# Retuning the cost table of a kernel's own list scheduler, and a second copy of its float32 scratch buffer

## The chip, the cores and the metric

The kernel runs on one core of a Trainium2 chip. The metric is the device time of one execution in microseconds (us). The core has five engines that this kernel uses: TensorE (PE) multiplies matrices, VectorE (DVE) and ScalarE (ACT) do elementwise work and read PSUM, GpSimd (POOL) does elementwise work in SBUF, and SyncE (SP) issues most DMAs; ACT issues the rest. Every engine works through its own instruction list in order, and the lists wait for each other by semaphores.

## What is computed

Two transformer layers over x (2 sequences of 1024 tokens, width 256, 16 heads of 16), with a context of 154 tokens:

```
# layer 0 (pre-norm)
h = ln1(x);  x = x + wo_sa(softmax(causal(rope(q(h)) rope(k(h)).T)) v(h))        # "sa"
h = ln2(x);  x = x + wo_ca(softmax(rope(q(h)) rope(k(ctx)).T) v(ctx))            # "ca"
h = ln3(x);  x = x + fc2(gelu_tanh(fc1(h)))
# layer 1
a = softmax(causal(q(x) k(ctx).T)) v(ctx)                                        # "la"
h = ln4(a + x);  out = h + W2(gelu(W1 h))
```

## The kernel before

**Tiling.** The 2 x 1024 tokens are cut into four chunks of 512 tokens (c = 0 to 3; two to a sequence). A chunk goes through stages made of small steps, and a step is a tuple such as ("proj", "qs", 3, 1). The steps that matter here:

- ("stats", norm, c, g): layer-norm statistics and scaling on DVE (L1156 to L1182); g = 1 carries the long part. ("tr", norm, c, g): the PE transposes the result (L854) and ACT copies it out.
- ("proj", kind, c, f): a projection of half the heads (f = 0 or 1); qs and ks are query and key of sa, qca the query of ca, qla that of la. PE multiplies (L881), ACT adds the bias into `rot` (L1303), DVE rotates it (not for qla) and splits it in bfloat16 parts (L1107 to L1117), POOL makes the third part (L1381). ("place", kind, c, f): SP issues six DMAs that lay the parts out by head in QA, KA or QC (L763). `rot` and `part` have two copies, so DVE, before it starts on the n-th projection, waits until the DMAs of the (n-2)-th have landed (`placed` in its list).
- ("max", att, c, hg, u): scores for the row maximum of a group of four heads (hg = 0 to 3): PE L968, then a DVE reduction L1200 from one of two PSUM banks. ("row", att, c, hg): the maxima are transposed (PE L982), rounded by DVE (L1211, L1212) and laid behind the queries by two small DMAs (SP, L770).
- ("exp", att, c, hg, g, h): scores once more with the maximum subtracted (L1001 or L1006, L1012 for la and ca) and the exponential on ACT (L1333). ("pv", ...): their product with the values into ps_o (L1043). ("evac", att, c, hg): ACT copies ps_o to `osb` (L1340). ("turn", att, c, hg): PE transposes osb (L1051), DVE divides (L1220, L1224).
- ("addatt", c, g): DVE adds la's result to x (L1138), ahead of ln4. ("lnout", c): DVE writes ln4's output (L1144, L1145).
- ("up", l, c, m) and ("down", l, c, m), m = 0 to 7: the two products of an MLP. The first is kept as float32r high and low halves: ACT computes the gelu twice (L1323 into `hid`, L1325 into `gel` in float32) and POOL subtracts (L1398). The input of an MLP is split in the same way in the tr steps of ln3 and ln4: ACT L1280 into `hup`, ACT L1287 into `gel`, POOL L1393. `gel` has one copy, so each ACT write of it waits until POOL has finished with the one before.

**What sets the order.** `order()` makes one list of 1721 steps, and each engine's instruction list is this list with the parts of other engines left out. It merges eleven threads of steps greedily: it keeps a running time per engine, adds the numbers of `COST` for each step (and of `LANDS` and `DMA_LATENCY` for what is landed later), asks `ready()` when the next step of each thread could start on PE, and takes the one with the least expected wait, ties going by `PRIORITY`. So a number in `COST` moves no work between engines. It changes what the scheduler believes of waits, and with that which steps stand beside which. The engines still wait by semaphores for what is really done.

Of the kernel before, what the change touches and what calls it, by code (L numbers as in the profile page):

```python
# [46 lines left out]
P = 128  # L47
B, LX, LY, E, H, FF = 2, 1024, 154, 256, 16, 1024
HD = E // H
CH = 512  # L50
# [5 lines left out]
KT = E // P  # L56
# [130 lines left out]
def split_weights():  # L187
# [10 lines left out]
    "wload": (("act", 0.6),), "wsave": (("act", 0.6),), "wsplit": (("act", 1.1), ("pool", 2.4)), "fetch": (("act", 2.4),),  # L198
    "stats": (("dve", 4.5),), "tr": (("pe", 0.6), ("act", 0.95)),
    "proj": (("pe", 1.9), ("act", 0.6), ("dve", 4.0)), "place": (("dma", 3.8),),  # L200
    "v": (("pe", 2.2), ("act", 0.55)), "wo": (("pe", 2.1), ("dve", 0.65)),
    "up": (("pe", 1.4), ("act", 1.4), ("pool", 1.3)), "down": (("pe", 1.41), ("act", 0.6)), "res": (("dve", 0.65),),
    "max": (("pe", 0.3), ("dve", 0.62)), "row": (("pe", 0.15), ("dve", 0.6), ("dma", 1.3)),
    "exp": (("pe", 0.25), ("act", 0.5)), "pv": (("pe", 1.0),), "evac": (("act", 0.5),),
    "turn": (("pe", 0.5), ("dve", 0.6)), "addatt": (("dve", 0.65),), "lnout": (("dve", 2.4),),
    "ctxk": (("pe", 1.3), ("act", 0.6), ("dve", 3.5), ("dma", 3.8)), "ctxv": (("pe", 2.6), ("act", 0.7)),
}
DMA_LATENCY = 2.2
LANDS = {"wload": 4.0, "wsave": 5.0, "fetch": 4.0}
LOW_LATER = 0.9  # L210
# [257 lines left out]
def build(nc, x, ctxT, sq, blocks, cols, rows, lnrow, ident, masks, trig, out):  # L468
# [14 lines left out]
    with ExitStack() as ctx:  # L483
# [40 lines left out]
        hT = sb("hT", [P, 2, KT, CH])  # L524
        gel = sb("gel", [P, CH])
        rot = sb("rot", [P, 2, CH])
# [33 lines left out]
        maskf = rot[:, :, :].rearrange("p a b -> p (a b)")[:, 0:MASKW]  # L560
        brow = gel[0:len(BIAS_ROWS), 0:E]
        bpart = [QC[0:len(BIAS_ROWS), i, 0:E] for i in range(3)]
# [665 lines left out]
        def _(act):  # L1228
# [12 lines left out]
            for s in ORDER:  # L1241
# [31 lines left out]
                if k == "tr":  # L1273
# [3 lines left out]
                    if what in ("ln3", "ln4"):  # L1277
                        half_of_input_free(act, s)
                        for f in range(KT):
                            act.activation(hup[:, 0, f, 2 * g * P:(2 * g + 2) * P], src[:, f, :], ACT.Identity,  # L1280
                                           bias=c0(what + "_b", f), scale=c0(what + "_g", f))
                        if low_nth[s] > 1:
                            act.wait_ge(s_low, low_nth[s] - 1)
                        dst = gel[:, :].rearrange("p (f n) -> p f n", f=KT)
                    if what in NORMS:
# [32 lines left out]
                elif k == "up":  # L1318
# [4 lines left out]
                    act.activation(hid[:, n % 2, 0, :], bank[:, :], gelu, bias=bias).then_inc(s_gelu, 1)  # L1323
                    act.wait_ge(s_low, low_nth[s] - 1)
                    act.activation(gel[:, :], bank[:, :], gelu, bias=bias).then_inc(s_chain_free[u % 2], 1)  # L1325
                elif k == "exp":
# [17 lines left out]
        def _(pool):  # L1344
# [22 lines left out]
            for s in ORDER:  # L1367
# [21 lines left out]
                elif k == "tr" and s[1] in ("ln3", "ln4"):  # L1389
                    cols = slice(2 * s[3] * P, (2 * s[3] + 2) * P)  # L1390
                    after_chain(pool, s)
                    half_of_input_free(pool, s)
                    pool.tensor_tensor(hup[:, 1, :, cols], gel[:, :].rearrange("p (f n) -> p f n", f=KT),  # L1393
                                       hup[:, 0, :, cols], ALU.subtract).then_inc(s_low, 1)
                elif k == "up":
                    n = up_nth[s]
                    after_chain(pool, s)
                    pool.tensor_tensor(hid[:, n % 2, 1, :], gel[:, :], hid[:, n % 2, 0, :],  # L1398
                                       ALU.subtract).then_inc(s_low, 1)
# [75 lines left out]
```

## Time and profile before

| | us |
|---|---|
| median of 3 runs | 1098.04 (1093.66 to 1100.06) |
| the profiled execution | 1102.32 |
| its span, first to last instruction | 1100.5 |
| PE busy | 902.2 (82%) |
| DVE busy | 599.0 (54%) |
| ACT busy | 481.1 (44%) |
| POOL busy | 174.4 (16%) |
| mean granted TensorE clock | 0.867 |

PE is busy for 82% of the span. Its time is what is to be explained: what stands in its list, and what it waits for. An idle stretch of another engine costs nothing by itself. A granted clock of 1.0 is TensorE's 2.4 GHz and 0.5 is 1.2 GHz; a value between is a mean over a stretch that had both.

### The profile page before, as it was taken

What the parts mean: (1) busy time and instruction counts of PE and PEld (TensorE: products, weight loads), DVE (VectorE), ACT (ScalarE), POOL (GpSimd) and SP (SyncE); (2) the same over time, 40 slices, a digit from 0 to 9 for tenths busy, and PEclk for the clock granted to TensorE, in tenths of its full rate; (3) what the DMA queues carried; (4) which work ended last, traced back from release to release, by engine and by line L of the source; (5) the groups of instructions that cost most, each with busy time, mean ns of one, the idle gap of its engine ahead of it and who ended that gap; (6) DMA issues with size and microseconds to landing.
All of it is one profiled execution on the core that took longest, in us unless ns stands there. A gap on an engine that the chain in (4) does not pass through costs nothing.

```text
span 1100.5 us, 14705 instructions
## 1 busy us (share of the span) xinstructions
PE 902.2 (82%) x5504; PEld 484.9 (44%) x5504; DVE 599.0 (54%) x1355; ACT 481.1 (44%) x926; POOL 174.4 (16%) x139
## 2 busy tenths in 40 slices
PE   2577877699889889878969886999886898898788
PEld 1233334244744256333337433743322473562377
DVE  3664764776467753368555777765206703515530
ACT  1224342145356555443443443256764444453543
POOL 4332000001300022001013101300000030230143
PEclk9768878598889989979889986999998798897888
DMA  8875343400640224239023602324003145062052
GB/s 301 231 207 140 50 89 57 58 2 20 163 59 14 28 53 139 32 69 112 2 29 110 102 3 29 116 77 59 2 20 41 18 131 81 26 158 30 1 173 96
DMA packets 60010, 86.08 MB, mean 78 GB/s; under 512 B 14726, under 2 KB 45602, under 8 KB 59938
## 3 DMA queue, kind: packets, MB, share of 16 engines
q1 hardware_dynamic: 46372, 38.99, 22.4%
q10 hardware_dynamic: 13568, 46.14, 12.3%
q8 instruction: 45, 0.74, 0.3%
q14 instruction: 25, 0.20, 0.1%
HBM read 47.08 MB, written 10.49 MB: 52 GB/s over the span
## 4 chain that ended last, share of the span: by engine, by line
PE 52%; DVE 14%; DMA 10%; ACT 9%; issue 8%; SPq 5%; POOL 2%; ACTq 0%; POOLq 0%; DVEq 0%
PE ps_o L1043 10%; PE ps_chain L905 8%; PE ps_max L968 7%; ACT probs L1333 5%; PE ps_exp L925 5%; PE ps_exp L1001 5%; DVE mcol L1200 5%; SPq L763 4%; DMA QA<-part 3%; PE ps_chain L881 3%; PE ps_exp L929 2%; PE ps_chain L889 2%; DMA QC<-part 2%; DMA stage<-in_blocks 2%; DVE swap L1107 2%
## 5 line engine op out<-in xcount | busy, mean ns | idle before, releaser
L1333 ACT ACTIVATE probs<-ps_exp 128x512 f32<-128x512 f32 (+3 forms) x544 | 261.2, 522 | 248.5 <-PE ps_exp L1006 88.5
L1200 DVE TENSOR_REDUCE mcol<-ps_max 128x3 f32<-128x462 f32 (+5 forms) x496 | 290.5, 625 | 123.2 <-PE ps_max L970 65.6
L968 PE MATMUL ps_max<-KA,QA 96*128 96x512 bf16 (+3 forms) x384 | 118.3, 360 | 53.5 <-DVE mcol L1200 28.2
L1001 PE MATMUL ps_exp<-QA,KA 98*128 98x512 bf16 (+3 forms) x384 | 119.1, 346 | 31.4 <-ACT probs L1333 24.9
L1381 POOL TENSOR_TENSOR part<-rot,part 128x512 bf16<-128x512 f32 (+1 forms) x36 | 40.5, 1126 | 568.4 <-DVE part L1117 568.4
L905 PE MATMUL ps_chain<-hup,ring 128*128 128x512 f32 x384 | 113.2, 436 | 3.7 <-ACT gel L1287 2.5
L1398 POOL TENSOR_TENSOR hid<-gel,hid 128x512 fp32r<-128x512 f32 x64 | 83.8, 1309 | 142.9 <-ACT gel L1325 142.9
L1323 ACT ACTIVATE hid<-ps_chain,col 128x512 fp32r<-128x512 f32 x64 | 44.1, 689 | 121.5 <-PE ps_chain L905 121.3
L1001 PEld LDWEIGHTS ps_exp<-QA,KA 98*128 98x128 bf16 x384 | 36.1, 99 | 125.6 <-ACT probs L1333 100.9
L1043 PE MATMUL ps_o<-probs,V 128*17 128x512 f32 (+3 forms) x768 | 85.8, 521 | 3.6 <-ACT probs L1333 2.6
L968 PEld LDWEIGHTS ps_max<-KA,QA 96*128 96x128 bf16 x384 | 37.4, 104 | 114.3 <-DVE mcol L1200 69.9
L905 PEld LDWEIGHTS ps_chain<-hup,ring 128*128 128x128 f32 x384 | 76.6, 210 | 22.1 <-issue 5.4
L1107 DVE TENSOR_TENSOR swap<-rot,sinT 64x512 f32<-64x512 f32 (+1 forms) x56 | 38.5, 688 | 85.6 <-ACT rot L1303 76.8
L925 PE MATMUL ps_exp<-ring,hid 128*128 128x256 f32 x512 | 76.8, 294 | 0.0
L925 PEld LDWEIGHTS ps_exp<-ring,hid 128*128 128x128 f32 x512 | 70.1, 195 | 6.5 <-issue 1.3
L970 PE MATMUL ps_max<-mask,idb 128*128 128x128 bf16 (+1 forms) x320 | 66.4, 235 | 0.0
L968 PE MATMUL ps_max<-KC,QC 96*128 96x154 bf16 x384 | 53.4, 253 | 12.6 <-DVE mcol L1200 7.9
L1004 PE MATMUL ps_exp<-mask,idb 128*128 128x128 bf16 x256 | 56.1, 229 | 0.0
L1303 ACT ACTIVATE rot<-ps_chain,col 128x512 f32<-128x512 f32 (+1 forms) x36 | 24.0, 669 | 64.6 <-PE ps_chain L881 54.0
L968 PEld LDWEIGHTS ps_max<-KC,QC 96*128 96x128 bf16 x384 | 31.8, 105 | 44.6 <-DVE mcol L1200 28.8
L1133 DVE TENSOR_TENSOR xb<-xb,ps_exp 128x512 f32<-128x512 f32 x16 | 10.2, 679 | 74.7 <-PE ps_exp L929 74.7
L1393 POOL TENSOR_TENSOR hup<-gel,hup 128x512 fp32r<-128x512 f32 x16 | 21.5, 1341 | 175.7 <-ACT gel L1287 175.7
(118 smaller groups left out, 1211.9 us busy)
## 6 DMA issues: line engine op xcount, KB each, us to landing
ring<-keep ACTq DMA_DIRECT2D x64, 512.0 KB, 3.3
QA<-part SPq DMA_DIRECT2D x72, 128.0 KB, 5.2
QC<-part SPq DMA_DIRECT2D x72, 128.0 KB, 5.2
keep<-ring ACTq DMA_DIRECT2D x8, 1024.0 KB, 5.3
KA<-part SPq DMA_DIRECT2D x48, 128.0 KB, 5.0
xb<-in_x SPq DMA_DIRECT2D x8, 512.0 KB, 6.2
stage<-in_blocks ACTq DMA_DIRECT2D x8, 512.0 KB, 8.6
out<-xb SPq DMA_DIRECT2D x4, 512.0 KB, 3.1
```

The lines of the kernel that those rows point to most:

```text
L905: mm = pe.matmul(bank[:, :], ring[:, n % RING, i, t * P:(t + 1) * P], hup[:, j, t, :], start=(i + j + t == 0), stop=(j + t == KT))
L925: pe.matmul(dst[t], hid[:, n % 2, 0, t * P:(t + 1) * P], ring[:, n % RING, j, 2 * P:4 * P], start=False, stop=False, skip_group_check=True)
L968: mm = pe.matmul(dst, q, kk, start=True, stop=not causal)
L970: mm = pe.matmul(bank[:, at0 + a0:at0 + a0 + w0], idb[:, :], mk, start=False, stop=True)
L1001: mm = pe.matmul(bank[:, q0:CH], KA[:, g // NT, hh, (g % NT) * P:(g % NT + 1) * P], QA[:, hh, q0:CH], start=True, stop=(r < 0))
L1004: mm = pe.matmul(bank[:, q0:q0 + P], idb[:, :], maskt, start=False, stop=True)
L1043: mm = pe.matmul(ps_o[p0:p0 + HD + 1, q0:CH], v, pr, start=first, stop=last, skip_group_check=True)
L1107: ins = dve.tensor_tensor(w[lo:lo + 64, a0:a0 + wd], r[hi:hi + 64, a0:a0 + wd], sinT[hi:hi + 64, t0:t0 + wd], ALU.mult)
L1200: dve.tensor_reduce(dst, src, AX.X, ALU.max).then_inc(s_max_done, 1)
L1323: act.activation(hid[:, n % 2, 0, :], bank[:, :], gelu, bias=bias).then_inc(s_gelu, 1)
L1333: act.activation(probs[:, n % 2, h, q0:CH], ps_exp[exp_nth[s] % 2][:, q0:CH], ACT.Exp).then_inc(s_exp_done, 1)
L1398: pool.tensor_tensor(hid[:, n % 2, 1, :], gel[:, :], hid[:, n % 2, 0, :], ALU.subtract).then_inc(s_low, 1)
```

## The change

It has two parts. The first edits the scheduler's numbers: a placing is now believed to land 1.3 us later (`LANDS`), a row of maxima 1.0 us earlier, and several durations go up or down by 0.05 to 0.5 us (`tr`, `proj`, `row`, `exp`, `evac`, `turn`). The second gives `gel` two copies, used in turn, so that ACT waits for the POOL subtraction before the last instead of the last. No instruction is added or taken away.

```diff
-    "stats": (("dve", 4.5),), "tr": (("pe", 0.6), ("act", 0.95)),
-    "proj": (("pe", 1.9), ("act", 0.6), ("dve", 4.0)), "place": (("dma", 3.8),),
+    "stats": (("dve", 4.5),), "tr": (("pe", 0.55), ("act", 1.15)),
+    "proj": (("pe", 1.8), ("act", 0.7), ("dve", 4.5)), "place": (("dma", 3.8),),
...
-    "max": (("pe", 0.3), ("dve", 0.62)), "row": (("pe", 0.15), ("dve", 0.6), ("dma", 1.3)),
-    "exp": (("pe", 0.25), ("act", 0.5)), "pv": (("pe", 1.0),), "evac": (("act", 0.5),),
-    "turn": (("pe", 0.5), ("dve", 0.6)), "addatt": (("dve", 0.65),), "lnout": (("dve", 2.4),),
+    "max": (("pe", 0.3), ("dve", 0.62)), "row": (("pe", 0.15), ("dve", 0.65), ("dma", 1.3)),
+    "exp": (("pe", 0.25), ("act", 0.56)), "pv": (("pe", 1.0),), "evac": (("act", 0.6),),
+    "turn": (("pe", 0.45), ("dve", 0.75)), "addatt": (("dve", 0.65),), "lnout": (("dve", 2.4),),
...
-LANDS = {"wload": 4.0, "wsave": 5.0, "fetch": 4.0}
+LANDS = {"place": 1.3, "ctxk": 1.3, "row": -1.0, "wload": 4.0, "wsave": 5.0, "fetch": 4.0}
...
-        gel = sb("gel", [P, CH])
+        gel = sb("gel", [P, 2, CH])
...
-                        if low_nth[s] > 1:
-                            act.wait_ge(s_low, low_nth[s] - 1)
-                        dst = gel[:, :].rearrange("p (f n) -> p f n", f=KT)
+                        if low_nth[s] > 2:
+                            act.wait_ge(s_low, low_nth[s] - 2)
+                        dst = gel[:, low_nth[s] % 2, :].rearrange("p (f n) -> p f n", f=KT)
...
-                    act.wait_ge(s_low, low_nth[s] - 1)
-                    act.activation(gel[:, :], bank[:, :], gelu, bias=bias).then_inc(s_chain_free[u % 2], 1)
+                    act.wait_ge(s_low, low_nth[s] - 2)
+                    act.activation(gel[:, low_nth[s] % 2, :], bank[:, :], gelu, bias=bias).then_inc(s_chain_free[u % 2], 1)
```

The first 27 steps of the list and one long stretch in the middle of chunk 2 and 3 stay as they were; elsewhere steps move by a few places, and at two places by much more.

**First place, PE, chunk 1's la attention.** Names: `w_sa_wq` marks the projection of sa's queries for chunk 3, second half, `w_l_wq` that of la's queries for chunk 1, `KC,QC 128x154` la's scores, `KA,QA` sa's, `idf,osb` a turn, `idf,mcol` a row, `idf,a_ctx` the transposes of ln4. Before, the projection stands behind the last of la's exps:

```order
L982 MATMUL ps_misc<-idf,mcol 16x128
L881 MATMUL ps_chain<-hT,w_sa_wq 128x512 x2
L1051 MATMUL ps_misc<-idf,osb 128x128 x4
L1012 MATMUL ps_exp<-QC,KC 32x512 x4
L1043 MATMUL ps_o<-probs,VA 17x512 x4
L1043 MATMUL ps_o<-probs,VB 17x512 x4
L1051 MATMUL ps_misc<-idf,osb 128x128 x4
L968 MATMUL ps_max<-KA,QA 128x128
```

Now it stands right behind the second projection of la's queries, and ahead of la's first scores:

```order
L881 MATMUL ps_chain<-hT,w_l_wq 128x512 x2
L982 MATMUL ps_misc<-idf,mcol 16x128
L881 MATMUL ps_chain<-hT,w_sa_wq 128x512 x2
L1051 MATMUL ps_misc<-idf,osb 128x128 x4
L968 MATMUL ps_max<-KC,QC 128x154 x16
L982 MATMUL ps_misc<-idf,mcol 16x128
L968 MATMUL ps_max<-KC,QC 128x154 x16
L1006 MATMUL ps_exp<-QC,KC 128x512 x2
L968 MATMUL ps_max<-KA,QA 128x128
```

The projection moved ahead by the whole of chunk 1's la attention, some 20 us of PE work.

**The same place on DVE, in the changed kernel.** `placed_qc0` is the landing of la's first queries, `max_ready` the scores:

```order
L1107 TENSOR_TENSOR swap<-rot,sinT 64x512 [waits chain_read1,placed_qc0]
L1107 TENSOR_TENSOR swap<-rot,sinT 64x512
L1111 TENSOR_TENSOR rot<-rot,cosT 128x512 [waits dve_chain]
L1113 TENSOR_TENSOR rot<-rot,swap 128x512 [waits dve_chain]
L1114 CAST part<-rot 128x512 [waits dve_chain]
L1116 TENSOR_TENSOR rot<-rot,part 128x512 [waits part0_ready]
L1117 CAST part<-rot 128x512 [waits dve_chain]
L1220 RECIPROCAL rec<-ps_misc 128x16 [waits misc_ready]
L1224 TENSOR_TENSOR a_sa<-ps_misc,rec 128x4x64 [waits dve_chain]
L1200 TENSOR_REDUCE mcol<-ps_max 128x3 [waits max_ready] x5
```

The rotation of the moved projection stands ahead of la's first reductions.

**Second place, PE, the end of the last attention.** Before, the first transposes (`idf,a_ctx`, ln4 of chunk 2) stand among the last products of chunk 3, and the MLP of chunk 2 follows:

```order
L1043 MATMUL ps_o<-probs,VA 17x512 x4
L854 MATMUL ps_chain<-idf,a_ctx 128x128 x4
L1051 MATMUL ps_misc<-idf,osb 128x128 x4
L854 MATMUL ps_chain<-idf,a_ctx 128x128 x4
L1043 MATMUL ps_o<-probs,VB 17x512 x4
L1051 MATMUL ps_misc<-idf,osb 128x128 x4
L905 MATMUL ps_chain<-hup,ring 128x512 x12
```

Now the last head group is one of chunk 2, and `idf,a_sa` is ln4 of chunk 3, whose MLP comes first:

```order
L1043 MATMUL ps_o<-probs,VA 17x512 x4
L1051 MATMUL ps_misc<-idf,osb 128x128 x4
L1043 MATMUL ps_o<-probs,VB 17x512 x4
L1051 MATMUL ps_misc<-idf,osb 128x128 x4
L854 MATMUL ps_chain<-idf,a_sa 128x128 x8
L905 MATMUL ps_chain<-hup,ring 128x512 x12
```

The MLPs of chunks 2 and 3 have changed places, and between the turn whose result ln4 needs and ln4's transposes stand one product and one turn.

## Rows read from the trace of the kernel before

**Rows 1.** The page: busy time of the engines, with shares and instructions.
```profile
PE 902.2 (82%) x5504; PEld 484.9 (44%) x5504; DVE 599.0 (54%) x1355; ACT 481.1 (44%) x926; POOL 174.4 (16%) x139
```
**Rows 2.** Waits of PE: who waited for whom, us in total, times, longest.
```profile
PE ps_max L968 <- DVE mcol L1200: 40.0, 74, 5.9
...
PE ps_max L968 <- DMA QA<-part: 24.8, 6, 6.5
...
PE ps_max L968 <- DMA QC<-part: 4.0, 4, 1.5
...
PE ps_exp L1001 <- DMA QA<-mrow: 2.4, 2, 2.0
...
PE ps_exp L1006 <- DMA QC<-mrow: 0.8, 1, 0.8
```
**Rows 3.** Windows: from:to, length, busy (instructions) of PE, PEld, DVE, ACT, POOL, clock, DMA.
```profile
550.00:577.50 27.50, 18.72 (x108) 10.17 (x109) 14.91 (x42) 12.34 (x26) 3.65 (x3) 0.81 0.22 30
660.00:687.50 27.50, 17.76 (x82) 9.16 (x81) 21.10 (x50) 8.95 (x16) 5.01 (x4) 0.61 0.22 29
```
**Rows 4.** Timeline, PE, products of up steps: start, us, ... xcount [idle before <-releaser].
```profile
418.51 1.55 PE L905 MATMUL ps_chain<-hup,ring 128*128 128x512 f32 x6
...
681.48 2.96 PE L905 MATMUL ps_chain<-hup,ring 128*128 128x512 f32 x6
```
**Rows 5.** Timeline, PE, the two longest waits of scores for placed queries in chunks 2, 3.
```profile
478.49 0.29 PE L968 MATMUL ps_max<-KA,QA 96*128 96x128 bf16 x1 [4.87 <-DMA QA<-part]
...
852.15 0.95 PE L968 MATMUL ps_max<-KC,QA 96*128 96x154 bf16 x6 [6.47 <-DMA QA<-part]
```
**Rows 6.** DMA issues: line, count, KB, median us from issue to landing.
```profile
QA<-mrow SPq DMA_DIRECT2D x48, 4.0 KB, 1.8
```
**Rows 7.** Timeline, the entry of chunk 1's first MLP.
```profile
570.66 1.15 POOL L1381 TENSOR_TENSOR part<-rot,part 128x512 bf16<-128x512 f32 x1 [55.18 <-DVE part L1117]
...
573.06 1.02 ACT L1287 ACTIVATE gel<-ps_chain,col 128x256 f32<-128x256 f32 x2 [3.73 <-POOL hup L1393]
...
574.41 0.39 PE L1001 MATMUL ps_exp<-QA,KA 98*128 98x256 bf16 x1 [7.17 <-ACT probs L1333]
```
**Rows 8.** Timeline, chunk 1's ln4 and the projection that the change moves.
```profile
658.05 2.01 PE L881 MATMUL ps_chain<-hT,w_sa_wq 128*128 128x512 f32 x4
...
664.26 3.84 SPq L763 DMA_DIRECT2D QA<-part  x6
...
666.14 1.09 PE L1051 MATMUL ps_misc<-idf,osb 128*128 128x128 f32 x4 [3.40 <-DVE a_ctx L1224]
...
672.89 0.29 PE L968 MATMUL ps_max<-KA,QA 96*128 96x128 bf16 x1 [5.66 <-DMA QA<-part]
...
673.70 1.38 DVE L1182 TENSOR_SCALAR a_ctx<-xb,mv,nw 128x256 f32<-128x256 f32 x4
```
**Rows 9.** Timeline, PE, chunk 1's first la queries and their first scores.
```profile
614.60 2.02 PE L881 MATMUL ps_chain<-hT,w_l_wq 128*128 128x512 f32 x4
...
626.91 0.58 PE L968 MATMUL ps_max<-KC,QC 96*128 96x154 bf16 x6 [0.64 <-DMA QC<-part]
```
**Rows 10.** Timeline, DVE, a rotation whose second-last placing had not landed.
```profile
509.76 1.39 DVE L1107 TENSOR_TENSOR swap<-rot,sinT 64x512 f32<-64x512 f32 x2 [1.69 <-DMA QC<-part]
```
**Rows 11.** Timeline, the end of the last attention and the second last MLP entry.
```profile
1037.38 1.11 PE L1051 MATMUL ps_misc<-idf,osb 128*128 128x128 f32 x4 [3.00 <-ACT osb L1340]
...
1049.46 2.45 DVE L1182 TENSOR_SCALAR a_sa<-xb,mv,nw 128x256 f32<-128x256 f32 x4
...
1066.31 1.17 PE L905 MATMUL ps_chain<-hup,ring 128*128 128x512 f32 x4 [2.52 <-ACT gel L1287]
...
1068.67 3.78 PE L905 MATMUL ps_chain<-hup,ring 128*128 128x512 f32 x8 [1.19 <-POOL hup L1393]
```
**Rows 12.** Waits of ACT for POOL.
```profile
ACT gel L1287 <- POOL hup L1393: 6.6, 7, 3.7
ACT gel L1325 <- POOL hid L1398: 4.9, 4, 2.9
```

More of the change, by code:

```diff
@@ L560, in build @@
         maskf = rot[:, :, :].rearrange("p a b -> p (a b)")[:, 0:MASKW]
-        brow = gel[0:len(BIAS_ROWS), 0:E]
+        brow = gel[0:len(BIAS_ROWS), 0, 0:E]
         bpart = [QC[0:len(BIAS_ROWS), i, 0:E] for i in range(3)]
@@ L1392, in _ @@
                     half_of_input_free(pool, s)
-                    pool.tensor_tensor(hup[:, 1, :, cols], gel[:, :].rearrange("p (f n) -> p f n", f=KT),
+                    pool.tensor_tensor(hup[:, 1, :, cols], gel[:, low_nth[s] % 2, :].rearrange("p (f n) -> p f n", f=KT),
                                        hup[:, 0, :, cols], ALU.subtract).then_inc(s_low, 1)
@@ L1397, in _ @@
                     after_chain(pool, s)
-                    pool.tensor_tensor(hid[:, n % 2, 1, :], gel[:, :], hid[:, n % 2, 0, :],
+                    pool.tensor_tensor(hid[:, n % 2, 1, :], gel[:, low_nth[s] % 2, :], hid[:, n % 2, 0, :],
                                        ALU.subtract).then_inc(s_low, 1)
```

## Prediction

> **What bounds the kernel now.** First the page's busy times: PE works 902.2 of 1100.5 us, no other engine over 55% [rows 1]. No instruction is added or removed, so the time moves only if PE's idle time or its clock moves. Second the waits of PE by releaser. The two large kinds are the DVE reduction of the score before (40.0 us in 74 small waits, inherent in two PSUM banks) and queries not yet placed: 24.8 us in 6 waits plus 4.0 in 4 [rows 2]. The rows of maxima are almost never waited for: 2.4 us in 2 waits plus 0.8 in 1 [rows 2]. Third the windows: around the two worst stalls the granted clock is 0.81 and 0.61, against 0.867 on the mean [rows 3]. So a stall costs twice, once as idle time and again as work at the lower of the two levels: six up products take 1.55 us in full flow and 2.96 behind the second stall [rows 4].
>
> For each wait I take how much PE work lies between a step and the step that needs it (the sum of PE's own times of the steps between, from this trace, in the old order and in the new). What does not cover the chain's length is idle time. These distances are my estimates.
>
> **1. Placings believed later.** The numbers now make the scheduler put 1.3 us more between a projection and its first scores. The distances grow: chunk 2's second sa projection from 14.6 to 16.8 us of work, where PE idles 4.87 now, so -2.2; chunk 3's ca projection from 6.0 to 6.9, idle 6.47, so -0.9 [rows 5]. The other places, all among the small waits of [rows 2]: chunk 2's first sa projection -1.0 (its whole wait), chunk 0's sa -0.8 and ca -0.5, la of chunks 0, 2 and 3 -0.4, -0.7 and -1.1. Sum: 3.1 + 1.0 + 1.3 + 2.2 = 7.6, so -7.6. Bounds: 0 (what moved in between is missing elsewhere) and -10.
>
> **2. Rows believed 1.0 us earlier.** The exps that read a row come closer behind it. A row's DMAs land 1.8 us after issue [rows 6], and the issue stands about 1.2 us behind PE's transposition, 3.0 in all; the nearest exps now stand at 2.5 to 3.9 us of work. Some ten of them could miss by up to 0.5 us, and others profit from being elsewhere. Bounds 0 and +3.2 (the present waits of this kind, doubled); I take +0.5, nearer to zero since most distances still cover.
>
> **3. Entry of chunk 1's first MLP.** Here PE stands 7.17 us because ACT is blocked 3.73 us before writing `gel`, behind two POOL operations, the first for a projection (570.66) [rows 7]. That projection is now about 6 us earlier, and with two copies ACT waits for neither. What is left is the chain transposition, four ACT copies, exp: about 1.8 of the 7.17. So -5.4. The stretch behind it runs at 0.81 [rows 3]; if it returned to nearly 1.0, 18.72 us of work would give back 3. Together -8.4, bounds -4 (only the 3.73 goes) and -10.
>
> **4. The moved projection (first place of the change).** It is `qs` of chunk 3, second half. It now stands 6.3 us of PE work behind the first la projection of chunk 1, with which it shares a copy of `rot`. From a la projection's end to its scores on PE passes 10.3 us (616.6 to 626.9) [rows 9]. So DVE waits for that landing, as it did for 1.69 us in the one such row [rows 10], until PE could be 10.3 us on; then it rotates for 4.5 us, until 14.8. La's reductions stand behind it in DVE's list, and PE has two banks, so PE stops at the third group of scores. And SP has the placing's six DMAs, 3.84 us of issue [rows 8], ahead of the rows of maxima. I get PE's first la exp at 21.3 us and the next scores at 22.3 against 10.9 us of work there: 11.4 idle, where now 3.9 are. Then ln4 of chunk 1: four reductions in between make its chain from turn to transposition 9.7 us, against 1.6 us of work that is left to cover it, since the projection and its scores have gone: about 8 idle. Now PE idles 3.40 ahead of the turn, which counts to the attention's 3.9, and 5.66 for the placed queries [rows 8], 5.8 with the small gaps beside it; that wait goes, and the statistics show in its place. Balance: 11.4 - 3.9 = +7.5 at la, 8 - 5.8 = +2 at ln4, +9.5 in all; and some 2 us of full-rate work more falls to the lower clock, which by the two rates of [rows 4] costs +2. So +11.5. Bounds: +3 (DVE catches up while PE has other steps, and the 5.66 pays for half) and +16 (both stalls whole, and 0.61 as granted clock over 27 us instead of 0.81 [rows 3]).
>
> **5. The end (second place).** ln4 of chunk 3 now comes first and right behind its turn: turn 0.8, addition 1.4, turn 0.7, statistics 5, transposition at 8.3, four ACT copies of 1.0 each, up products at 12.9, against 2.9 us of work: 10 idle. Now 3.00 is lost there [rows 11]. So +7, and 1.5 for the clock. The last evacuation stands ahead of the last exp on ACT, -1.2. The second entry loses 2.52 and 1.19 now [rows 11], waiting for `gel` and the subtraction; with two copies most of that goes, and with the clock I take -4. Sum +3.3, bounds -3 and +8. The statistics here take 1.38 us for the last four operations if POOL is quiet, as in [rows 8], and 2.45 if it is not, as in [rows 11]; POOL should be quiet, as the other chunk's MLP is not running.
>
> That difference fits the Trainium skill, page "SBUF — State Buffer", section "Who interferes with whom": DVE's two-port modes and GpSimd take the same pair of ports in turns. By that page alone the stall at the end would be the shorter of the two; the sum is the same.
>
> **6. Output layer norm and chunk 3's ln3.** The work between chunk 3's output projection and its transposition falls from 5.1 to 1.3 us: 4.8 idle for 1.7, less 1.5 for la waits of chunk 2 that it takes the place of: +1.6. Elsewhere small moves of 0.3 to 1.0 us, -2.7 in all, bounds -5 and +2.
>
> **7. Two copies elsewhere.** ACT's waits for POOL at `gel` are 6.6 and 4.9 us in the whole span [rows 12], the 3.73 of part 3 among them. In the flow of an MLP PE never waits for them, so I cost the rest at nothing; what hides it is PE's work on 18 products a step. The float32r subtraction keeps its own place on POOL.
>
> **Sum.** -7.6 + 0.5 - 8.4 + 11.5 + 3.3 + 1.6 - 2.7 = -1.8 us. From the profiled execution, 1102.3, that gives 1100.5. That execution stood 4.3 over the median of the runs, 1098.0, so the median would be 1096.2, rounded to 1096.5.
>
> **Rivals.** *A, the forecast:* gains and losses cancel. *B, the moved projection is covered.* If DVE's wait ends before PE runs out of la scores (the other steps there, a turn and sa scores, use DVE little) part 4 is +3, and if ln4 of chunk 3 at the end finds its turn early, part 5 is 0: -1.8 - 8.5 - 3.3 = -13.6, median 1084. For it: DVE is only 54% busy [rows 1], so the stretch around may leave it slack. Against: both projections share one copy, and 6.3 is less than 10.3. *C, DVE is blocked for its full length.* The wait for la's first landing, behind the moved projection, decides as soon as that landing is later than PE's third group of la scores; then part 4 is +16 and, with part 5 at +8 by the same pattern of an exposed norm, the sum is +7.4, median about 1105.5. For it: the clock of 0.61 after just such a stall [rows 3]. Against: the distances may be larger than I sum, since PE works slower at the lower clock and so covers more. *D, the numbers do nothing real:* the gains of part 1 are taken back at the next wait for a reduction, since DVE's 40.0 us stay [rows 2]; then the sum is -1.8 + 7.6 = +5.8, median 1104, at the slow bound of no change.
>
> On the clock the Trainium skill, page "TensorE: Matmul & The Clock Gate", section "HAM oscillation — how this bites in real kernels", says that an array left waiting between bursts falls to its low clock, so that each burst begins slow. The two rates in [rows 4] agree. Without the clock's terms (-3 in part 3, +2 in part 4, +1.5 and some -1.5 in part 5) the sum would be -0.8, nearly the same; with new stalls of 8 to 11 us the page speaks for C.
>
> **How the numbers follow.** A measurement of this kernel can tell about 0.5%, 5.5 us, from no change: 1092.5 to 1103.5. Chances: A 0.36, B 0.34, C 0.20, D 0.10. A's own spread is some 5 us, so 0.06 of it lies below the middle and 0.03 above. B reaches into the middle with 0.04, C with 0.02, and D lies half in it. Faster 0.06 + 0.30 = 0.36, same 0.27 + 0.04 + 0.02 + 0.05 = 0.38, slower 0.03 + 0.18 + 0.05 = 0.26. The independent bounds of parts 1, 3, 4 and 5 give about +-12 us; the range takes B's 1084 with 2 us and C's 1105.5 with the outer bound of part 4: 1082 to 1114.
>
> **What would show it.** Right for 1: the waits of `ps_max` for QA and QC fall from 28.8 us to below 20. For 3: no idle time over 3 us at chunk 1's first MLP entry. For 4: DVE waits several us for QC's placing ahead of a rotation in chunk 1's la attention, and PE waits for `mcol` there over 5 us; a granted clock near 0.6 behind it. For 5: 8 to 11 us of idle PE ahead of the last `a_sa` transpositions, statistics at 1.38. For 7: ACT's waits for POOL fall from 11.5 to under 3. Wrong it would be if DVE never waits at the moved projection (B), or if idle time at it exceeds 15 us (C), or if the waits for placings fall and those for `mcol` rise by as much (D).

## The result: slower by 1.8%, outside the range

The changed kernel takes 1116.9 us (median of 4 runs, 1110.48 to 1119.29) against 1096.01 us for the kernel before in the same comparison. The ratio is 1.0177, interval [1.0121, 1.0234]. The forecast was 1096.5 in a range of 1082 to 1114. The nearest rival, C (DVE blocked behind the moved projection), named 1105.5.

### The profile page after: what moved, and what is told of

Read it like the earlier page. It is cut to its first block, busy times and chain, and to the rows that moved or that the text cites. A ratio compares the mean times of both kernels' runs of the same rounds, so it can differ in the third digit from the quotient of the medians.

```text
span 1116.5 us, 14707 instructions
## 1 busy us (share of the span) xinstructions
PE 907.6 (81%) x5504; PEld 487.6 (44%) x5504; DVE 601.2 (54%) x1355; ACT 478.6 (43%) x926; POOL 175.9 (16%) x139
## 4 chain that ended last, share of the span: by engine, by line
PE 55%; DVE 17%; DMA 10%; ACT 9%; SPq 4%; issue 3%; POOL 1%; ACTq 0%; POOLq 0%; DVEq 0%
PE ps_o L1043 11%; PE ps_max L968 8%; PE ps_chain L905 8%; DVE mcol L1200 6%; ACT probs L1333 5%; PE ps_exp L1001 5%; PE ps_exp L925 4%; PE ps_chain L881 4%; PE ps_chain L889 3%; SPq L763 3%; DMA QA<-part 3%; PE ps_exp L929 2%; PE ps_exp L1006 2%; PE ps_chain L854 2%; DMA stage<-in_blocks 2%
## 5 line engine op out<-in xcount | busy, mean ns | idle before, releaser
L1200 DVE TENSOR_REDUCE mcol<-ps_max 128x1 f32<-128x512 f32 (+5 forms) x496 | 291.9, 626 | 121.7 <-PE ps_max L968 60.3
L968 PE MATMUL ps_max<-KA,QA 96*128 96x512 bf16 (+3 forms) x384 | 121.6, 365 | 45.5 <-DVE mcol L1200 28.9
L905 PE MATMUL ps_chain<-hup,ring 128*128 128x512 f32 x384 | 109.1, 424 | 8.0 <-ACT gel L1287 5.1
L1398 POOL TENSOR_TENSOR hid<-gel,hid 128x512 fp32r<-128x512 f32 x64 | 85.7, 1340 | 139.7 <-ACT gel L1325 139.7
L968 PEld LDWEIGHTS ps_max<-KA,QA 96*128 96x128 bf16 x384 | 38.7, 105 | 106.6 <-DVE mcol L1200 75.2
L1043 PE MATMUL ps_o<-probs,V 128*17 128x512 f32 (+3 forms) x768 | 82.3, 501 | 3.1 <-ACT probs L1333 2.8
L905 PEld LDWEIGHTS ps_chain<-hup,ring 128*128 128x128 f32 x384 | 73.3, 201 | 24.3 <-issue 6.5
L968 PE MATMUL ps_max<-KC,QC 96*128 96x154 bf16 x384 | 55.3, 259 | 14.8 <-DVE mcol L1200 11.7
L968 PEld LDWEIGHTS ps_max<-KC,QC 96*128 96x128 bf16 x384 | 32.6, 107 | 47.4 <-DVE mcol L1200 34.7
L1220 DVE RECIPROCAL rec<-ps_misc 128x16 f32<-128x16 f32 x48 | 12.2, 253 | 74.5 <-PE ps_misc L1051 74.4
```

Source lines behind the costliest of these rows:

```text
L905: mm = pe.matmul(bank[:, :], ring[:, n % RING, i, t * P:(t + 1) * P], hup[:, j, t, :], start=(i + j + t == 0), stop=(j + t == KT))
L968: mm = pe.matmul(dst, q, kk, start=True, stop=not causal)
L1043: mm = pe.matmul(ps_o[p0:p0 + HD + 1, q0:CH], v, pr, start=first, stop=last, skip_group_check=True)
L1200: dve.tensor_reduce(dst, src, AX.X, ALU.max).then_inc(s_max_done, 1)
L1398: pool.tensor_tensor(hid[:, n % 2, 1, :], gel[:, low_nth[s] % 2, :], hid[:, n % 2, 0, :], ALU.subtract).then_inc(s_low, 1)
```

## The profile after

First the page's busy times and PE's waits by releaser, as in [rows 1] and [rows 2]; columns as there.

```profile
span 1116.5 us, 14707 instructions
...
PE 907.6 (81%) x5504; PEld 487.6 (44%) x5504; DVE 601.2 (54%) x1355; ACT 478.6 (43%) x926; POOL 175.9 (16%) x139
```
```profile
PE ps_max L968 <- DVE mcol L1200: 44.6, 70, 6.0
...
PE ps_chain L854 <- DVE a_ctx L1182: 12.0, 3, 4.5
...
PE ps_chain L854 <- DVE a_sa L1182: 9.6, 2, 5.8
PE ps_max L968 <- DMA QA<-part: 9.2, 4, 4.8
PE ps_exp L1001 <- DMA QA<-mrow: 7.4, 1, 7.4
...
PE ps_max L968 <- DMA QC<-part: 2.9, 3, 1.4
```

The edit does what it says: the waits for placed queries fell from 28.8 us [rows 2] to 9.2 + 2.9 = 12.1. The time went elsewhere: 44.6 for 40.0 on the reductions, 7.4 for 2.4 on a row, and two lines for the statistics of ln2, ln3 and ln4 (12.0 and 9.6, where the trace of before has 4.4 and none).

The largest of the waits that fell, 6.47 us ahead of chunk 3's first ca scores [rows 5], only changed its name. A transposition of chunk 2's ca result now stands ahead of these scores, and waits 5.05 us for a divide that DVE does behind the rotation of the same projection (PE and DVE, start, us, instruction, [idle before <- releaser]):

```profile
845.26 0.63 PE L1051 MATMUL ps_misc<-idf,osb 128*128 128x128 f32 x4 [0.32 <-DVE a_ctx L1224]
...
849.83 0.43 DVE L1117 CAST part<-rot 128x512 bf16<-128x512 f32 x1
...
850.46 0.42 DVE L1224 TENSOR_TENSOR a_ctx<-ps_misc,rec 128x256 f32<-128x256 f32 x1
850.94 1.11 PE L854 MATMUL ps_chain<-idf,a_ctx 128*128 128x128 f32 x4 [5.05 <-DVE a_ctx L1224]
852.36 0.95 PE L968 MATMUL ps_max<-KC,QA 96*128 96x154 bf16 x6 [0.30 <-DMA QA<-part]
```

From the end of that turn to the scores pass 6.5 us, as before; one transposition of 1.11 us has moved into the gap.

The place of the moved projection, chunk 1's la: timeline, PE and DVE (start, us, instruction, [idle before <- releaser]).

```profile
620.02 0.28 PE L982 MATMUL ps_misc<-idf,mcol 128*16 128x128 f32 x1 [2.58 <-DVE mcol L1208]
620.14 3.64 PE L881 MATMUL ps_chain<-hT,w_sa_wq 128*128 128x512 f32 x4
...
624.05 0.56 PE L968 MATMUL ps_max<-KC,QC 96*128 96x154 bf16 x6
624.60 1.39 DVE L1107 TENSOR_TENSOR swap<-rot,sinT 64x512 f32<-64x512 f32 x2 [3.67 <-ACT rot L1303]
...
629.63 3.46 DVE L1200 TENSOR_REDUCE mcol<-ps_max 128x3 f32<-128x462 f32 x6
630.32 1.11 PE L968 MATMUL ps_max<-KC,QC 96*128 96x154 bf16 x6 [5.70 <-DVE mcol L1200]
...
675.54 1.76 PE L854 MATMUL ps_chain<-idf,a_ctx 128*128 128x128 f32 x7 [4.17 <-DVE a_ctx L1182]
```

The first la scores are there at 624.05, but DVE rotates the moved projection until 629.1 and then divides for a turn before it reduces them, and PE stands 5.70 us. What the prediction had wrong is visible too: DVE's rotation was released by ACT's `rot`, not by a landing. Against [rows 8] the same projection takes 3.64 us instead of 2.01: it runs at about half the rate behind the 2.58 us wait.

The end of the last attention, as in [rows 11].

```profile
1043.34 0.66 PE L1051 MATMUL ps_misc<-idf,osb 128*128 128x128 f32 x4
...
1051.31 1.38 DVE L1182 TENSOR_SCALAR a_sa<-xb,mv,nw 128x256 f32<-128x256 f32 x4
1052.11 1.97 PE L854 MATMUL ps_chain<-idf,a_sa 128*128 128x128 f32 x8 [5.76 <-DVE a_sa L1182]
...
1055.97 1.05 ACT L1287 ACTIVATE gel<-ps_chain,col 128x256 f32<-128x256 f32 x2
...
1057.11 1.19 PE L905 MATMUL ps_chain<-hup,ring 128*128 128x512 f32 x2 [3.04 <-ACT gel L1287]
```

From the turn of chunk 3 to its first up product pass 13.8 us, for which the prediction said 12.9. The statistics took 1.38, as said for a quiet POOL. Windows (from:to, length, busy of PE, PEld, DVE, ACT, POOL, granted clock, DMA): the first is la of chunks 2 and 3 in the changed kernel, the second the same microseconds before.

```profile
990.00:1028.00 38.00, 32.21 (x159) 11.60 (x161) 16.25 (x36) 10.54 (x19) 0.00 (x0) 0.53 0.16 17
```
```profile
990.00:1028.00 38.00, 29.83 (x201) 10.33 (x204) 22.32 (x63) 14.81 (x28) 0.00 (x0) 0.83 0.22 23
```

PE is busier and does fewer instructions, 159 instead of 201: 38 us almost wholly at the lower level. No part of the prediction had this.

## The experiments

The lists of steps before and after hold the same steps up to three points: step 848 (chunk 1's last ca scores), step 1189 (chunk 3's first sa products) and step 1412 (chunk 3's first ca scores). So the old and the new list can be joined there. Where such a joined list is used, both lists are computed by the file's own scheduler (`old` with the numbers of before, `new` with those of after), and all lines of the profile behind `order()` are 28 to 35 higher (L996, L997 or L1003 is L968 of before). "Two copies" is the change's second part, which all kernels have but e0 and e2. Reference for most is e1: two copies and nothing else.

**e1: two copies, old list.**

```diff
-LANDS = {"place": 1.3, "ctxk": 1.3, "row": -1.0, "wload": 4.0, "wsave": 5.0, "fetch": 4.0}
+LANDS = {"wload": 4.0, "wsave": 5.0, "fetch": 4.0}
```
(and `COST` as before)

> The second part alone: two copies of gel, the list of steps as before. Theory (the changed kernel loses at the moved projection and at the end, and gains at chunk 1's first MLP entry by both parts together): only ACT's 3.73 us wait and the second entry's 2.52 and 1.19 go, so -4 to -7 us against before, 1089 to 1092. Rival (the second copy gives nothing, since PE stands for ACT's work itself and POOL's projection step stays in front of the subtraction): within 2 us of before. Either way the idle stretch of 7.17 us ahead of the exps of chunk 2 shortens to about 3.5 by the theory and stays at 7 by the rival.

Measured: 1082.54 us, ratio 0.9876 [0.9852, 0.9900], -12.4 us. It is the fastest kernel of the study, and the change's second half alone. The gain is larger than the 4 to 7 us of the theory.

**e0: the kernel before once more.** No edit.

> The kernel before once more, for a trace of the same day as the others. The record of before shows a granted clock of 0.95 in its undisturbed stretches, and those of all kernels since show 1.00. Theory (that is a property of the one recorded execution): now 1.00, with a time of 1091 to 1099 and a span some 7 us below the first record. Rival (it belongs to this list of steps): 0.95 again.

Measured, in one run: 1095.06 us, span 1093.2, clock 0.907. The first record was a long execution with a clock of 0.867; where it shows 0.93 from 290 to 390 us, this one shows 0.97 and 1.4 us less PE time (from 960 to 980 us it is 0.95 and 1.00). So the theory holds.

```profile
290.00:390.00 100.00, 90.50 (x643) 41.47 (x642) 70.82 (x147) 56.01 (x110) 7.73 (x7) 0.93 0.31 54
```
```profile
290.00:390.00 100.00, 89.12 (x650) 40.08 (x648) 71.30 (x151) 56.14 (x110) 7.23 (x6) 0.97 0.29 49
```

So the traces from here on are compared with e0 and e1. Chunk 1's first MLP entry, e0 (ACT, PE), then e1 (ACT, PE):

```profile
567.50 1.02 ACT L1287 ACTIVATE gel<-ps_chain,col 128x256 f32<-128x256 f32 x2 [3.87 <-POOL hup L1393]
...
568.85 0.39 PE L1001 MATMUL ps_exp<-QA,KA 98*128 98x256 bf16 x1 [7.33 <-ACT probs L1333]
```
```profile
563.45 1.04 ACT L1287 ACTIVATE gel<-ps_chain,col 128x256 f32<-128x256 f32 x2
...
564.82 0.28 PE L1001 MATMUL ps_exp<-QA,KA 98*128 98x256 bf16 x1 [3.34 <-ACT probs L1333]
```

ACT's wait of 3.87 is gone and PE's falls by 3.99; PE waits 1.63 us for placed queries 8 us later, where e0 doesn't. ACT's waits for POOL at `gel` are 6.7, 6.5 and 0.5 us in e0, and none is left in e1:

```profile
ACT gel L1287 <- POOL hup L1393: 6.7, 7, 3.9
ACT gel L1325 <- POOL hid L1398: 6.5, 7, 2.9
```
```profile
ACT rot L1303 <- POOL part L1381: 2.3, 1, 2.3
ACT VA L1312 <- POOL ring L1387: 2.0, 1, 2.0
ACT hT L1287 <- POOL ring L1387: 0.9, 1, 0.9
```

The two spans differ by 10.9 us. By the pages PE's idle time (span less busy) is 200.0 and 191.0 us, its busy time 893.2 and 891.3. By place the picture is another. Of the idle time 5.1 us lie between 480 and 680 us, but PE's own time there is 4.7 longer in e1, so that e1 is ahead by only 2.8 us at step 1583, in the middle of chunk 2's la. The other 8.1 us come behind it: 1.6 of idle time, mostly at the last MLP's entry, 1.6 in the last MLP (25.6 us of PE time in e0, 24.0 in e1) and 4.9 in la of chunks 2 and 3, where e0 ran partly at the lower level (granted clock 0.66 from 980 to 1000 us). No step there writes `gel`, and e0 is one execution, so it is not shown that this last part belongs to the second copy. The first record of before is as slow behind step 1583 (109.7 us, e0 111.0, e1 102.9).

```profile
980.00:1000.00 20.00, 16.80 (x98) 7.47 (x98) 10.56 (x24) 6.21 (x12) 1.16 (x1) 0.66 0.49 52
```

**e2: new list, one copy.** `COST` and `LANDS` of after, everything else of before.

> The first part alone: the new list of steps, one copy of gel. Theory: in the new list the projection is 6 us earlier and POOL free at chunk 1's entry, so one copy costs there at most 1 us, but at the two last entries 2 to 3 each: +3 to +6 us against the changed kernel, about 1121. Rival (the whole gain at chunk 1's entry was the second copy): +8 to +10 against the changed kernel, about 1126.

Measured: 1114.18 us, ratio 1.0166 [1.0136, 1.0195], not to be told from the changed kernel; theory and rival both said more. So in the new list the second copy is worth nothing that can be told, where it gives 12.4 us in the old one. The trace says why for chunk 1's entry: with the new list and one copy, ACT's longest waits at `gel` are 1.5 and 0.5 us, since the projection that held POOL stands 6 us earlier. There both parts of the change went for the same wait. Why nothing of the rest is left is not shown.

```profile
ACT gel L1325 <- POOL hid L1398: 3.8, 5, 1.5
ACT gel L1287 <- POOL hup L1393: 3.3, 7, 0.5
```

**e5, e3, e4: the new list in one stretch only.**

```diff
+    return new[:848] + old[848:]                   # e5
+    return old[:848] + new[848:1189] + old[1189:]  # e3
+    return old[:1412] + new[1412:]                 # e4
```

> Two copies of gel, the new list up to step 848 (chunk 1's last ca scores, where both lists hold the same steps), the old list behind it. It holds nearly all of the retimed placings of part 1 of the prediction but neither the moved projection nor the new end. Theory A (the prediction's part 1 stands, 4 to 6 us are gained by placings no longer waited for): 1077 to 1079. Theory B (what is gained at the placings is given back at other waits in the same stretch, since against the kernel with two copies alone the changed kernel's trace has 2 to 3 us more idle time there): within 2 us of it, 1081 to 1085.

> Two copies of gel, the old list with steps 848 to 1189 of the new one: chunk 3's first query projection ahead of chunk 1's ln3, and the moved projection; first part and end are the old ones. Theory (the moved projection costs what the changed kernel's trace loses against the kernel with two copies alone, 16 to 18 us from chunk 1's la queries to chunk 2's ln2, less the 5 gained ahead): +9 to +13 against the kernel with two copies alone, 1092 to 1096. Rival (rotation, placing and rows waited for are mostly covered, as the case B of the prediction, and undoing it gave only 7): +2 to +5, 1085 to 1088.

> Two copies of gel, the list of before up to chunk 3's first ca scores (step 1412, where both lists hold the same steps) and the new list from there. Theory 1 (the end costs by itself): the trace of the changed kernel loses 15 us against before from there on, 7.5 at ln3 of chunk 3, 6 in la of chunks 2 and 3 at the low clock, and 10 at the exit less the 3 that the second copy gives. So +12 to +17 against the kernel with two copies alone. Rival (the losses at the end follow from the clock that the earlier stretch leaves behind, not from the list): under +8, the low stretch at la of chunks 2 and 3 missing and only the exit's idle time there.

| | us | ratio to before | against e1 |
|---|---|---|---|
| e5, first stretch | 1084.92 | 0.9920 [0.9890, 0.9949] | +2.4 |
| e3, middle | 1097.59 | 1.0019 [0.9991, 1.0047] | +15.0 |
| e4, end | 1107.23 | 1.0101 [1.0074, 1.0129] | +24.7 |
| changed kernel | 1116.9 | 1.0177 [1.0121, 1.0234] | +34.4 |

The last column is a difference of medians; e5 was timed on another chip than e1, and by the ratios the four are +4.8, +15.7, +24.6 and +33.0, each good to some 4 us. e5 is what theory B said, e3 lies 2 us and e4 8 us above their theories. The middle and the end lose.

The traces say where. The table has the time on PE of each stretch, in one execution of each kernel, between the steps at which the lists can be joined (e8 and e12 are described below; at step 1583 the new list differs by one step):

| | to 848 | to 1189 | to 1412 | to 1583 | to the end |
|---|---|---|---|---|---|
| e0, before | 534.8 | 199.6 | 102.6 | 140.7 | 111.0 |
| e1, two copies | 534.8 | 197.9 | 102.6 | 139.6 | 102.9 |
| e5, first stretch | 532.4 | 200.5 | 102.6 | 140.1 | 103.1 |
| e3, middle | 533.3 | 211.7 | 103.4 | 140.0 | 103.1 |
| e8, placing's number | 529.5 | 214.4 | 103.3 | 143.4 | 102.9 |
| e4, end | 534.5 | 198.5 | 102.5 | 142.1 | 124.2 |
| e12, exit | 534.8 | 197.7 | 102.6 | 139.7 | 114.4 |
| changed kernel | 533.3 | 209.8 | 102.8 | 142.0 | 124.2 |

In the changed kernel the differences to e1 are -1.5, +11.9, +0.2, +2.4 and +21.3, and their sum is the whole. The three differences of the table above sum to 42, 8 more: e5 shows +2.4 for that -1.5, e3 +15.0 for 11.9, e4 24.7 for 23.7. e5 is 2.4 us ahead at step 848 and loses it by step 1189, over steps that stand as in e1. So the retimed placings gain nothing that lasts (theory B).

In e5 and in the changed kernel one place shows how the gain is given back, chunk 0's last sa group. The timeline of SP's queue and of PE, first of the changed kernel:

```profile
148.83 4.46 SPq L757 DMA_DIRECT2D KC<-part  x6
153.33 1.25 SPq L770 DMA_DIRECT2D QA<-mrow  x2
```
```profile
155.74 0.61 PE L1001 MATMUL ps_exp<-QA,KA 98*128 98x512 bf16 x1 [7.41 <-DMA QA<-mrow]
```

And of e0, SP's queue and PE:

```profile
148.93 3.97 SPq L757 DMA_DIRECT2D KC<-part  x6
152.94 1.25 SPq L770 DMA_DIRECT2D QA<-mrow  x2
```
```profile
150.42 1.09 PE L1051 MATMUL ps_misc<-idf,osb 128*128 128x128 f32 x4 [2.27 <-DVE mrow L1212]
155.35 0.61 PE L1001 MATMUL ps_exp<-QA,KA 98*128 98x512 bf16 x1 [1.79 <-DMA QA<-mrow]
```

The row's DMAs stand in SP's queue behind six of the context's keys, in both kernels, and SP gets to them at the same time. PE has done 3 us more of its list by then, waits 0.72 + 7.41 instead of 2.27 + 1.79, and goes on at 155.74 instead of 155.35.

In e3 the rows of the moved projection are those of the changed kernel: waits of 2.58 and 4.92 us in la and 4.16 at ln4. Taking out the steps that only stand in another order, e3 is 7 us ahead of e1 at 595 us and 12 us behind at 743, so the stretch with the moved projection costs 19 to 20 us, some 14 of it idle time. That is gross: part of it takes back the 7 us gained ahead of it.

**e6, e7: the moved projection undone at step 1003.**

```diff
+    head = new[:1003]
+    return head + [s for s in old[:1189] if s not in head] + new[1189:]   # e6
+    return head + [s for s in old if s not in head]                       # e7
```

> The changed kernel with the first place undone: behind chunk 1's second la projection the list of before is followed up to step 1189, where both lists hold the same steps, and then the new one again. Theory 1 (the moved projection is the loss): the changed kernel's trace loses 16 us from there to chunk 2's ln2 against before; DVE does not wait for QC's placing ahead of a rotation, the idle 5.70 and 2.58 us are gone, and the time is 12 to 16 us below the changed kernel, about 1103. Rival (the stretch is lost to the clock in any case, as before with 0.61): at most 5 us below, 1112 or more.

> Two copies of gel, the new list up to chunk 1's second la projection (step 1003), the old one behind it: the moved projection and the new end are both undone. Theory 1 (these two places are the whole loss): below the kernel with two copies alone by what the stretch ahead gains in the changed kernel's trace, 5 to 8 us by chunk 1's first MLP, so 1075 to 1079. Rival (the time is lost again at the joint, since the projection then waits for its turn behind la as before): 1082 to 1088.

Measured: e6 1109.82 us (1096.82 to 1114.38 in 10 runs), ratio 1.0093 [1.0058, 1.0128], 7 below the changed kernel (9 by the ratios) instead of 12 to 16; e7 1086.04, ratio 0.9926 [0.9897, 0.9955], 3.5 above e1 (5.5 by the ratios) instead of 3 to 7 below, as its rival said. The joint has a fault of its own, as e7's timeline shows below: the new list has used up chunk 3's scores by step 1003, and nothing is left to cover the placing of la's queries.

```profile
620.16 0.95 PE L997 MATMUL ps_max<-KC,QC 96*128 96x154 bf16 x6 [5.42 <-DMA QC<-part]
```

The 5.70 us are replaced by 5.42. So these two don't give the price of the moved projection, and e3 gives it only together with this: e7, with the projection at its old place, is 10 us ahead of e1 at step 1003 and 1 us ahead at step 1189, so it loses 9 us there, where e3 loses 19. The gain ahead of that point, visible in the traces of e3 and of the changed kernel too, is borrowed: it comes from having spent that cover. The moved projection by itself costs between 10 and 20 us; no run parts it from the rest.

**e8: of all numbers only the placing's.**

```diff
-LANDS = {"wload": 4.0, "wsave": 5.0, "fetch": 4.0}
+LANDS = {"place": 1.3, "ctxk": 1.3, "wload": 4.0, "wsave": 5.0, "fetch": 4.0}
```

> Two copies of gel and of all numbers only the 1.3 us for a placing. Its list has the moved projection but the old end (MLP of chunk 2 first). Theory (the placing's number brings the moved projection, other numbers the new end, and the new end is the larger loss): 1085 to 1095, well below the changed kernel. Rival (any list with placings believed later loses as much by new waits for reductions): 1105 or more.

Measured: 1100.97 us (1093.67 to 1107.34), ratio 1.0046 [1.0009, 1.0083], between the two expectations: 18.4 above e1. Its list moves the projection too, but is the old one from step 1583 on, and its trace is 16.5 us behind e1's between steps 848 and 1189 and equal to it at the end (table above). So the placing's number alone brings the middle's loss, and the end's needs the other numbers.

**e12, e9, e10, e11: the end taken apart.** e12 has the old list up to the last turn of chunk 3 and behind it chunk 3's ln4 and MLP first; e9 takes the new list from step 1583, in the middle of chunk 2's la; e10 has only steps 1412 to 1583 of the new one; e11 is e4 with the exps, products, evacuation and turn of chunk 2's last la group behind chunk 3's statistics.

```diff
+    first = [s for s in old[:old.index(("turn", "la", 3, 3)) + 1] if s[:3] != ("tr", "ln4", 2)]
+    return first + [s for s in new if s not in first]                     # e12
+    head = old[:1583]
+    return head + [s for s in new if s not in head]                       # e9
+    head = old[:1412] + new[1412:1583]
+    return head + [s for s in old if s not in head]                       # e10
+    both = old[:1412] + new[1412:]                                        # e11
+    last = [s for s in both if s[:4] == ("exp", "la", 2, 3) or s[:4] == ("pv", "la", 2, 3)]
+    rest = [s for s in both if s not in last]
+    for s in (("evac", "la", 2, 3), ("turn", "la", 2, 3)):
+        rest.remove(s)
+        last.append(s)
+    i = rest.index(("stats", "ln4", 3, 1)) + 1
+    return rest[:i] + last + rest[i:]
```

> Two copies of gel, the old list up to the last turn of la in chunk 3, only without chunk 2's ln4 transpositions, and behind it chunk 3's statistics, transpositions and MLP first and chunk 2's last: the exit exposed by itself, with chunk 2's and 3's la as in the old list. Theory (the new end costs twice: the exposed ln4 chain, about 10 us idle, and apart from it 11.5 us of la work more at the low clock, which comes from the new interleaving of chunks 2 and 3): +9 to +12 against the kernel with two copies alone, 1092 to 1095, and la of chunks 2 and 3 keeps its 52 us of PE time. Rival (the exit is the whole loss of 24 us, the low clock being its companion): 1103 to 1108.

> Two copies of gel, the old list up to step 1583, in the middle of chunk 2's la attention, the new one behind it: chunk 3's la ahead of chunk 2's last group, and the MLP of chunk 3 first. Theory (the exit of the last attention is exposed as part 5 says, with 10 us idle): +10 to +14 against the kernel with two copies alone, 1093 to 1097. Rival (the exit costs only together with the low clock of the attention ahead of it, which the steps before 1583 bring): under +6, 1088 or less.

> Two copies of gel, the old list with steps 1412 to 1583 of the new one: chunk 3's ln3 with 1.3 us of work ahead of its transposition instead of 5.1, and chunk 2's la queries and scores around it; the end is the old one. Theory (the stretch costs what its own trace shows, 5 us of idle time at ln3 and 3 around it): +7 to +9 against the kernel with two copies alone, about 1090. Rival (the prediction's +1.6): 1084. If this and the run with the new end alone add up to the 25 us of both together, the two are independent; if they fall 5 us or more short of it, the two meet in the low clock of chunk 3's la attention.

> The kernel with the new end alone, and in it one thing changed: the exps and products of chunk 2's last la group stand behind the turn, the addition and the statistics of chunk 3, so that some 4 us of work cover ln4's chain. Theory (the exposed chain is most of the loss at the end): the 5.8 us of idle time ahead of the transposition fall to 1 or 2, and the time falls by 4 to 6 us against the new end alone, to about 1102. Rival (most of the loss is the low clock in chunk 3's la attention ahead of it, which this doesn't touch): under 2 us, 1105 or more; a low clock of 0.50 between 985 and 1025 us of the trace stays in either case.

| | us | ratio to before | against e1 |
|---|---|---|---|
| e12, exit alone | 1096.08 | 1.0000 [0.9970, 1.0031] | +13.5 |
| e10, ln3 and la of chunk 2 | 1085.47 | 0.9918 [0.9887, 0.9948] | +2.9 |
| e9, from step 1583 | 1108.58 | 1.0123 [1.0072, 1.0174] | +26.0 |
| e11, e4 with the exit covered | 1101.95 | 1.0067 [1.0043, 1.0091] | +19.4 |

e9, e10 and e12 were timed on other chips than e1; by the ratios they are 27.0, 4.6 and 13.6 above it. e12 lies 1.5 us above its theory, far from its rival; e10 is at its rival's value and not at its theory's; e9 is far above both.

The exit by itself costs 13.5 of e4's 24.7 us. In e12's timeline of PE it is idle time:

```profile
1021.98 0.66 PE L1080 MATMUL ps_misc<-idf,osb 128*128 128x128 f32 x4 [0.72 <-ACT osb L1369]
1029.90 1.97 PE L883 MATMUL ps_chain<-idf,a_sa 128*128 128x128 f32 x8 [7.26 <-DVE a_sa L1211]
1034.90 1.62 PE L934 MATMUL ps_chain<-hup,ring 128*128 128x512 f32 x3 [3.04 <-ACT gel L1316]
```

That is 11.0 us, where e1 waits 2.48. The other 11 are the clock in la of chunks 2 and 3. PE's own time in all steps of these two stages, summed from the traces, is 52.3 us in e1, 52.4 in e12, 63.8 in e4 and in the changed kernel (64.1 in e11). With the old interleaving it is 52.3 to 54.0 in six executions and 58.0 in e0, with either half of the new one 54.0 (e10) and 58.7 (e9). The windows of e12 first, then e4:

```profile
980.00:1000.00 20.00, 14.77 (x120) 6.42 (x124) 14.55 (x32) 6.62 (x12) 0.00 (x0) 0.97 0.33 36
1000.00:1020.00 20.00, 15.62 (x96) 4.41 (x89) 8.94 (x34) 9.76 (x18) 0.00 (x0) 0.86 0.01 1
```
```profile
980.00:1000.00 20.00, 17.13 (x91) 6.88 (x91) 11.32 (x24) 4.58 (x9) 0.00 (x0) 0.55 0.29 31
1000.00:1020.00 20.00, 17.36 (x78) 4.96 (x74) 5.62 (x14) 5.69 (x11) 0.00 (x0) 0.51 0.00 1
```

So the low clock does not belong to the exit; most of it comes with the new interleaving of the two chunks. e10, which has the first half of it, loses little. e9 has the second half but brings a wait of 5.49 us of its own for chunk 3's placed queries at the joint, so it can't price that half. e11 covers the chain with 4 us of work: the wait for ln4's statistics falls from 5.76 to 1.16, and the time by 5.3 us, as its theory says for this step; the low clock stays. That the exposed chain is most of the loss at the end, which the same theory says, does not hold: the two are of one size. The row of e11's timeline:

```profile
1037.63 1.30 PE L889 MATMUL ps_chain<-idf,a_sa 128*128 128x128 f32 x8 [1.16 <-DVE a_sa L1217]
```

## Why the prediction was wrong, point by point

The forecast was -1.8 us; the span of the changed kernel is 23.3 us above e0's. By stretch, with the parts that can be placed (the rest, +0.5 of part 2 and -2.7 of small moves, can't):

| | said | changed kernel against e0 |
|---|---|---|
| to step 848 (part 1's waits there) | -4.9 | -1.5 |
| to step 1189 (parts 3 and 4) | +3.1 | +10.2 |
| to the end (part 1's other waits, parts 5 and 6) | +2.2 | +14.7 |

- **Part 1, -7.6: failed.** The waits for placings fell (in e5 from 32.1 us in e1 to 27.1, and at chunk 2's second sa projection by the 2.2 said), but e5 as a whole is at +2.4. The step that failed is taking each wait's shortening as time gained. The next wait takes it up: in chunk 0 behind it stands a DVE and SP chain that is not moved, and PE only comes to it earlier (155.35 and 155.74 us); at chunk 3's ca the 6.47 became 5.05 + 0.30.
- **Part 2, +0.5.** The waits for rows rose from 3.2 us to 7.4 + 1.6, beyond the upper bound of +3.2. But the 7.41 is the wait just named, which also takes the place of another 2.27. No run has the row's number alone; its price is open.
- **Part 3, -8.4.** Right in mechanism and place. In e1 the second copy takes 3.99 of the 7.33, as the bound of 3.73 said; in the changed kernel the gap is gone. The 3 us of clock are not seen in e1: PE's own time from step 848 to 1003 is 77.4 us in e0 and 77.7 in e1. And e2 shows that the two parts are alternatives there, and e7 that the earlier projection is paid for at la's queries. Part 7 priced the second copy elsewhere at nothing; in the old list it brings 12.4 us in all, against some 8 by parts 3 and 5.
- **Part 4, +11.5: right in sign; with part 3 it gives +3.1, and the stretch lost 10.2.** In e3's trace it is 19 to 20 gross, beyond the bound of 16, of which some 9 are lost in e7 too, where the projection has its old place; so whether the part by itself was within its bounds is open. DVE's wait for QC's placing, from which the price was worked out, did not occur; what blocks is the rotation itself, on DVE from 624.60 to 629.0. Missing in the sum are the 2.58 ahead of the projection, its run at half rate (3.64 for 2.01) and the wait of 3.40 for chunk 2's ln2 later (3.54 in e3), where e0 and e1 have none over 1 us.
- **Part 5, +3.3: the chain was right, 9.5 us of idle time in the changed kernel for 10 said.** The term was mis-sized twice. The exit costs 13.5 (e12), not 7 + 1.5 - 1.2. And the -4 for the second entry was too much: two copies leave 2.02 and 0.58 of the 3.71 there. The 11.5 us of la work at the low clock (63.8 for 52.3) were in no term; this is the largest single miss.
- **Part 6, +1.6 for ln3: +2.9 in e10 (4.6 by the ratios),** near the outer end of what a comparison of this size can tell. The idle time ahead of ln3's transposition is 3.83 us in the changed kernel, for 4.8 said.
- **The rivals.** The cases took their sum from part 1's gain and added clock in small lumps. Without part 1, by the prediction's other terms alone, the forecast is +5.8, rival D's 1104, which had 0.10. D's mechanism, a gain taken back at the next wait, holds. Of C's, DVE is blocked by the rotation and not by a landing. Neither rival has the low clock in la, and neither gives 1117.
- **The record.** The trace of before was an execution 7 us above the later median and at a lower clock. The long waits that the prediction used are in e0 again within 0.6 us, so this moved no step. Two readings were off and carry no term: the second window of [rows 3] is not at one of the two worst stalls (6.47 us at 852 [rows 5] is longer than its 5.66), and 1096.2 was rounded up to 1096.5.

What stays open: why the granted clock stays at its lower level in la of chunks 2 and 3 with the new interleaving and not with the old. From 980 to 1020 us neither has a wait over 1.5 us (e4 and e1). Also open is what the second copy gives behind step 1583, beyond the 3.2 us at and in the last MLP, and what the moved projection costs by itself.

## What to carry to other kernels

A wait that is removed is worth only the distance to the next thing that is already late on the same chain; follow that chain (DVE, then SP's queue) before the gain is booked. Where a scheduler's numbers change, look first for the largest move, and ask whose turn on DVE it takes: 4.5 us of rotation ahead of the reductions that PE needs held PE for 5.70 us at one place, and the retimed placings saved nothing that lasted. A cheap structural edit (a second buffer) is to be timed apart from a retuning: here it gives 12.4 us alone and nothing together with the new numbers, which the joint change, slower by 21 us, could not show.

## What the runs showed of the hardware

TensorE's granted clock can stay at its lower level while PE is busy: 0.53 over 38 us with 32.21 us of PE time and no wait over 1.34 us in it. It fell 2 us behind a wait of 0.99 us for placed queries (1.00 until 992 us, 0.50 from 993); e1 waits 1.37 us at 981 us for the same queries and keeps 1.00 until 998. In this stretch it was worth 11.5 us, as much as the 11.0 us that the exit stands still in e12. The same list of steps also ran with a clock of 0.867 in one execution and 0.907 in another, with 9 us less PE time (902.2 and 893.2), where idle time hardly differed. Runs of one list differ with the clock: e6's fastest took 1096.82 us at 0.910 and its slowest 1114.38 at 0.890.
